# Score tiles of 16 positions of all 8 heads in place of 128 positions of one head

## The reference

```
xn  = layernorm(x)
q   = (xn @ Wq + bq).reshape(B, T, 8, 128) + pe        # T = 1024, B = 8
k,v = split(xn @ Wkv + bkv);  k = k + pe               # one head, shared by all 8
s   = where(causal, q @ k.T / sqrt(128), min)
out = (softmax(s) @ v).reshape(B, T, 1024) @ Wo
ffn = sigmoid(xr @ Wr.T) * (relu(xk @ Wk.T)**2 @ Wv.T) # xr, xk mix xn with the position before
y   = x + out + ffn
```

## Time and profile before

| | us |
|---|---|
| median of 3 runs (1758.52 to 1759.99) | 1759.03 |
| span of the profiled execution | 1756.4 |
| TensorE busy | 1686.9 (96%) |
| weight loads busy | 1624.8 (93%) |
| VectorE busy | 1244.0 (71%) |
| ScalarE busy | 1118.1 (64%) |
| GpSimd busy | 784.9 (45%) |

### The profile page before, as it was taken

The page is one execution under the profiler, slowest core; times in us unless marked ns, Lnnn a source line. Parts: engine busy times, 40 slices in busy tenths (PEclk is TensorE's granted clock), DMA queues, the critical chain, the costliest instruction groups (busy, mean ns, idle before and its releaser), DMA issues.

```text
span 1756.4 us, 41996 instructions
## 1 busy us (share of the span) xinstructions
PE 1686.9 (96%) x12982; PEld 1624.8 (93%) x12982; DVE 1244.0 (71%) x3466; ACT 1118.1 (64%) x2694; POOL 784.9 (45%) x991
## 2 busy tenths in 40 slices
PE   5999999999999998999989999899998999989999
PEld 5899988999899998999989999899998999989998
DVE  5777757777677766777767767677766777667776
ACT  4666656765566656676566766666666666666665
POOL 5544345443454434544345443454435443444434
PEclk9999999999999999999999999999999999999999
DMA  3000000000000000000000000000000000000000
GB/s 123 14 13 5 10 15 14 14 5 13 12 14 14 6 12 13 17 11 13 4 15 14 11 13 4 16 13 14 10 4 15 13 14 10 4 20 12 11 11 13
DMA packets 23586, 25.38 MB, mean 14 GB/s; under 512 B 2064, under 2 KB 22672, under 8 KB 23312
## 3 DMA queue, kind: packets, MB, share of 16 engines
q1 hardware_dynamic: 22736, 21.50, 3.9%
q10 hardware_dynamic: 576, 0.66, 0.1%
HBM read 13.77 MB, written 8.39 MB: 13 GB/s over the span
## 4 chain that ended last, share of the span: by engine, by line
PE 92%; issue 3%; DVE 2%; POOL 1%; ACT 1%; DMA 1%; SPq 0%; POOLq 0%; DVEq 0%; ACTq 0%
PE pS L741 33%; PE pO L741 22%; PE pG L741 21%; PE pT L851 15%; POOL X L348 1%; DMA X<-wq_dram 1%; DVE X L709 0%; ACT pt L464 0%; PE pS L787 0%; PE pG L787 0%; DVE pt L643 0%; DVE qtmp L588 0%; PE pG L797 0%; DVE rec L716 0%; PE pS L797 0%
## 5 line engine op out<-in xcount | busy, mean ns | idle before, releaser
L348 POOL TENSOR_SCALAR X<-X,rec 128x128 f32<-128x128 f32 (+7 forms) x518 | 385.9, 745 | 952.0 <-DVE rec L716 951.5
L741 PE MATMUL pS<-kt,qt 128*128 128x512 f32 (+5 forms) x2325 | 513.4, 348 | 0.8 <-POOL qt L332 0.8
L643 DVE TENSOR_TENSOR pt<-pT,pt 128x512 fp32r<-128x512 f32 (+3 forms) x772 | 402.7, 549 | 112.0 <-ACT pt L464 97.6
L741 PE MATMUL pO<-pt,v 128*128 128x256 f32 x3459 | 451.5, 280 | 0.0
L709 DVE CUSTOM_DVE_ANT_0 X<-pS,mask 128x128 f32<-128x128 f32 (+7 forms) x519 | 387.4, 746 | 79.9 <-PE pS L741 72.2
L741 PEld LDWEIGHTS pO<-pt,v 128*128 128x128 f32 x3459 | 436.8, 188 | 6.7
L472 ACT ACTIVATE X<-X,bias 128x128 f32<-128x128 f32 (+7 forms) x518 | 404.7, 781 | 28.8 <-DVE bias L709 28.3
L464 ACT CAST pt<-pT 128x512 fp32r<-128x512 f32 (+3 forms) x772 | 343.5, 480 | 102.7 <-PE pT L851 94.9
L741 PEld LDWEIGHTS pS<-kt,qt 128*128 128x128 f32 x2325 | 376.3, 190 | 19.2 <-POOL qt L332 1.0
L851 PE MATMUL pT<-ident,X 128*128 128x128 f32 x2308 | 343.9, 275 | 52.0 <-POOL X L348 26.8
L851 PEld LDWEIGHTS pT<-ident,X 128*128 128x128 f32 x2308 | 267.4, 141 | 86.6 <-issue 30.4
(11 more groups left out here) (90 smaller groups left out, 1583.1 us busy)
## 6 DMA issues: line engine op xcount, KB each, us to landing
xtok<-x_dram SPq DMA_DIRECT2D x36, 256.0 KB, 2.7
out_dram<-xtok SPq DMA_DIRECT2D x64, 128.0 KB, 1.7
X<-wq_dram SPq DMA_DIRECT2D x2, 512.0 KB, 8.5
X<-wo_dram SPq DMA_DIRECT2D x2, 512.0 KB, 3.9
pet<-pet_dram ACTq DMA_DIRECT2D x1, 512.0 KB, 6.5
kpos<-petok_dram SPq DMA_DIRECT2D x1, 512.0 KB, 9.2
X<-wkv_dram SPq DMA_DIRECT2D x1, 256.0 KB, 3.7
X<-wk_dram SPq DMA_DIRECT2D x1, 256.0 KB, 9.5
```

What stands on the lines that cost most here:

```text
L348: nc.gpsimd.tensor_scalar(X[:, j, 0:w], X[:, j, 0:w], rec[:, j:j + 1], 1.0, ALU.mult, ALU.mult).then_inc(normed, 1)
L643: nc.vector.tensor_tensor(pt[1][:, (s // 2) % 2, k:k + nk, half_q], pT[u % 2][:, 0:nk * P].rearrange("p (k q) -> p k q", k=nk), pt[0][:, ( ...
L741: last = nc.tensor.matmul(out, a[i], m[j], start=start and k == 0, stop=k == n - 1)
```

## The change

A step is now 16 positions (`SUB`) of all 8 heads: 128 rows again, since keys and values are shared. Step s has the width qi*128 + (s % 8 + 1)*16, so the last tile's columns are taken only as far as its own positions; from qi 4 on the two halves are half of that each. `qt` is laid out by groups of 16 positions, heads inside, so that the 128 weights of a step are contiguous; the ScalarE cast and the GpSimd subtract write it in runs of 16 elements, and `ot` likewise. A step needs the queries of all heads, and the Q units are moved ahead accordingly: all four pairs of a chunk are made in the chunk before, and before the loop for the first. GpSimd zeroes the columns between the width and the end of the tile, because the transposes still take whole blocks; then it multiplies, in turn it + 2 in place of it + 1.

The transposes stand 5 steps behind the scores, the value products 8, LEAD is 9. `X` has five rows, and the four first steps of an entry use narrow rows of their own (`Xn`), so the mask no longer waits for transposes. The keys and values get a buffer of their own (`kv`), apart from `xn`. The other fillers change turns.

The order inside a turn changes on two engines. On ScalarE the exp of it - 1 moves from behind the casts of the transposes to the front of the turn. On VectorE the reciprocal of it - 1 moves from behind the mask of it to between the subtracts and the fillers. The small triangle is built from a 128 x 8 x 16 pattern once at the start. The DMA scratch is set smaller.

```diff
 NC = T // CHUNK
 NT = T // P
 PAIRS = H // 2
+SUB = P // H
 STEPS = NT * H
 SCALE = float(D) ** -0.5
 EPS = 1e-5
 MASKED = 1e30
 HUGE = 3e38
-T_LAG = 3
-PV_LAG = 6
-XBUF = 4
+T_LAG = 5
+PV_LAG = 8
+XBUF = 5
+NARROW = 4
 MIX_AT = 12
-LEAD = 7
+LEAD = 9
 LAST_IT = STEPS + LEAD
 PER = TPC * H
 def fillers():
     at = {it: [] for it in range(LAST_IT)}
     for c in range(NC):
-        turns = {2: ("FK", c, 0), 4: ("Q", c, 3), 7: ("XT", c + 1, 0), 8: ("FV", c, 0),
-                 9: ("KV", c + 1, 0), 10: ("Q", c + 1, 0), 11: ("KT", c + 1, 0), 12: ("Q", c + 1, 1),
-                 13: ("WO", c, 0), 14: ("Q", c + 1, 2)}
+        turns = {1: ("FK", c, 0), 4: ("FR", c, 0), 5: ("XT", c + 1, 0), 6: ("FV", c, 0),
+                 7: ("KV", c + 1, 0), 8: ("Q", c + 1, 0), 9: ("KT", c + 1, 0), 10: ("Q", c + 1, 1),
+                 11: ("Q", c + 1, 2), 13: ("Q", c + 1, 3), 15: ("WO", c, 0)}
         if c == NC - 1:
-            turns = {2: ("FK", c, 0), 4: ("Q", c, 3), 7: ("XT", c + 1, 0), 8: ("FV", c, 0),
-                     9: ("KV", c + 1, 0), 11: ("Q", c + 1, 0), 12: ("Q", c + 1, 1), 13: ("WO", c, 0),
-                     14: ("Q", c + 1, 2), 15: ("KT", c + 1, 0)}
+            turns = {i: u for i, u in turns.items() if u[0] not in ("KT", "WO")} | {14: ("WO", c, 0), 15: ("KT", c + 1, 0)}
         for i, u in sorted(turns.items()):
             at[c * PER + i].append(u)
-        at[c * PER + PER + 5].append(("WO", c, 1))
     for c in range(NC):
-        at[c * PER + 6].append(("FR", c, 0))
+        at[c * PER + PER + 7].append(("WO", c, 1))
     return at
 FILL = fillers()
-START = [("XT", 0, 0), ("KV", 0, 0), ("KT", 0, 0)] + [("Q", 0, p) for p in range(PAIRS - 1)]
+START = [("XT", 0, 0), ("KV", 0, 0), ("KT", 0, 0)] + [("Q", 0, p) for p in range(PAIRS)]
+def slot_of(s):
+    return XBUF + s if s < NARROW else (s - NARROW) % XBUF
+def width(s):
+    return s // H * P + (s % H + 1) * SUB
...
-        qt = [sb(f"qt{i}", [P, 2, H, CHUNK], R) for i in range(2)]
+        qt = [sb(f"qt{i}", [P, 2, CHUNK // SUB, H, SUB], R) for i in range(2)]
...
-        bias = sb("bias", [P, XBUF])
-        total = sb("total", [P, XBUF])
-        rec = sb("rec", [P, XBUF])
+        Xn = sb("Xn", [P, NARROW, P])
+        bias = sb("bias", [P, XBUF + NARROW])
+        total = sb("total", [P, XBUF + NARROW])
+        rec = sb("rec", [P, XBUF + NARROW])
...
-            tri = mask[:, T - P:T]
-            nc.gpsimd.affine_select(out=tri, in_=tri, compare_op=ALU.is_ge, fill=MASKED,
-                                    base=0, pattern=[[-1, P]], channel_multiplier=1).then_inc(consts, 1)
+            nc.gpsimd.memset(steps_of[:, :, :], MASKED).then_inc(tri_made, 1)
+            pool.wait_ge(tri_made, 1)
+            nc.gpsimd.affine_select(out=steps_of[:, :, :], in_=steps_of[:, :, :], compare_op=ALU.is_ge, fill=0.0,
+                                    base=0, pattern=[[-SUB, H], [0, SUB]], channel_multiplier=1
+                                    ).then_inc(tri_made, 1)
+            pool.wait_ge(tri_made, 2)
+            nc.gpsimd.affine_select(out=steps_of[:, :, :], in_=steps_of[:, :, :], compare_op=ALU.is_ge, fill=0.0,
+                                    base=SUB - 1, pattern=[[SUB, H], [0, SUB]], channel_multiplier=-1
+                                    ).then_inc(tri_made, 1)
+            pool.wait_ge(tri_made, 3)
+            nc.gpsimd.affine_select(out=steps_of[:, :, :], in_=steps_of[:, :, :], compare_op=ALU.is_gt, fill=0.0,
+                                    base=0, pattern=[[SUB, H], [1, SUB]], channel_multiplier=-1
+                                    ).then_inc(tri_made, 1)
...
             def turn(b, it):
-                s = it - 1
+                s = it - 2
                 if 0 <= s < STEPS:
-
-                    w = (s // H + 1) * P
-                    j = s % XBUF
+                    w = width(s)
+                    j = slot_of(s)
                     pool.wait_ge(rec_ready, b * STEPS + s + 1)
                     pool.sem_inc(pool_passed, 1)
-                    nc.gpsimd.tensor_scalar(X[:, j, 0:w], X[:, j, 0:w], rec[:, j:j + 1], 1.0,
+                    if s % H < H - 1:
+                        nc.gpsimd.memset(x_row(s, w, (s // H + 1) * P), 0.0).then_inc(normed, 1)
+                    nc.gpsimd.tensor_scalar(x_row(s, 0, w), x_row(s, 0, w), rec[:, j:j + 1], 1.0,
                                             ALU.mult, ALU.mult).then_inc(normed, 1)
...
             def turn(b, it):
+                s = it - 1
+                if 0 <= s < STEPS:
+                    w = width(s)
+                    j = slot_of(s)
+                    act.wait_ge(masked, b * STEPS + s + 1)
+                    nc.scalar.activation(x_row(s, 0, w), x_row(s, 0, w), ACT.Exp, bias=bias[:, j:j + 1],
+                                         scale=-1.0, accum_out=total[:, j:j + 1]).then_inc(exp_done, 1)
                 first = it - PV_LAG
                 if 0 <= first < STEPS and first % 2 == 0:
                     pair = first // 2
                     act.wait_ge(pv_done, b * (STEPS // 2) + pair + 1)
-                    h = first % H
-                    if h == 0 and not (isinstance(b, int) and pair == 0):
+                    q0 = first % H * SUB
+                    if q0 == 0 and not (isinstance(b, int) and pair == 0):
 
                         act.wait_ge(filled["WO"], b * NT + first // H)
-                    nc.scalar.copy(ot[0][:, h:h + 2, :],
-                                   pO[:, 0:2 * P].rearrange("p (h q) -> p h q", h=2)).then_inc(o_hi, 1)
+                    nc.scalar.copy(ot[0][:, :, q0:q0 + 2 * SUB].rearrange("p h (t q) -> p t h q", t=2),
+                                   pO[:, 0:2 * P].rearrange("p (t h q) -> p t h q", t=2, h=H)).then_inc(o_hi, 1)
...
-                s = it - 1
-                if 0 <= s < STEPS:
-                    w = (s // H + 1) * P
-                    j = s % XBUF
-                    act.wait_ge(masked, b * STEPS + s + 1)
-                    nc.scalar.activation(X[:, j, 0:w], X[:, j, 0:w], ACT.Exp, bias=bias[:, j:j + 1],
-                                         scale=-1.0, accum_out=total[:, j:j + 1]).then_inc(exp_done, 1)
...
+                s = it - 1
+                if 0 <= s < STEPS:
+                    j = slot_of(s)
+                    dve.wait_ge(exp_done, b * STEPS + s + 1)
+                    nc.vector.reciprocal(rec[:, j:j + 1], total[:, j:j + 1]).then_inc(rec_ready, 1)
...
-                    w = (qi + 1) * P
-                    j = s % XBUF
+                    w = width(s)
+                    j = slot_of(s)
 
                     if qi < 4:
                         scores = pS[s % 2][:, 0, 0:w]
                         m = mask[:, T - w:T]
-                        o = X[:, j, 0:w]
+                        o = x_row(s, 0, w)
                     else:
                         scores = pS[s % 2][:, :, 0:w // 2]
                         m = mask[:, T - w:T].rearrange("p (a n) -> p a n", a=2)
-                        o = X[:, j, 0:w].rearrange("p (a n) -> p a n", a=2)
-                    if s >= XBUF:
-                        dve.wait_ge(t_filled, b * T_BODY + T_FIRST[s - XBUF + 1])
-                    elif not first_row:
-                        dve.wait_ge(t_filled, (b - 1) * T_BODY + T_FIRST[STEPS + s - XBUF + 1])
+                        o = x_row(s, 0, w).rearrange("p (a n) -> p a n", a=2)
                     dve.wait_ge(s_filled, b * STEPS + s + 1)
                     dve.sem_inc(dve_passed, 1)
                     nc.vector.tensor_tensor_reduce(out=o, in0=scores, in1=m, scale=SCALE, scalar=HUGE,
                                                    op0=ALU.add, op1=ALU.min,
                                                    accum_out=bias[:, j:j + 1]).then_inc(masked, 1)
-                s = it - 1
-                if 0 <= s < STEPS:
-                    j = s % XBUF
...
-                    pe.wait_ge(normed, b * STEPS + s + 1)
+                    pe.wait_ge(normed, b * N_BODY + N_FIRST[s + 1])
...
-                    qi, h = s // H, s % H
-                    c, t = qi // TPC, qi % TPC
-                    w = (qi + 1) * P
+                    qi = s // H
+                    c = qi // TPC
+                    w = width(s)
                     n = chunk_no(b, c)
                     if s % PER == 0:
                         pe.wait_ge(kt_ready, n + 1)
-                    if t == 0:
-                        pe.wait_ge(q_ready, n * H + h + 1)
+                        pe.wait_ge(q_ready, n * H + H)
                     if s >= 2 or not first_row:
                         pe.wait_ge(masked, b * STEPS + s - 1)
                     if SHARED <= s < SHARED + 2:
...
-                                       [([q[:, c % 2, h, t * P:(t + 1) * P] for q in qt],
+                                       [([q[:, c % 2, s % PER, :, :].rearrange("p h q -> p (h q)")
+                                         for q in qt],
```

74 lines of the change are left out of this document (45 added, 29 removed).

## The result

| | before | after |
|---|---|---|
| median, us | 1759.03 (3 runs, 1758.52 to 1759.99) | 2179.2 (4 runs, 2178.19 to 2180.59) |
| ratio, 95% interval | | 1.2387 (1.2368 to 1.2405) |
| span of the profiled execution | 1756.4 | 2177.1 |
| granted clock, mean of that execution | 0.992 | 0.937 |

A fourth execution of the kernel before took 3341.32 us; it is in neither the median nor the ratio. The changed kernel takes 420 us more. The prediction had the direction and the mechanism, 2013 us with a range of 1890 to 2090; the time lies 89 us above the top of the range and 166 above the forecast.

What follows compares the result with a forecast made beforehand. The prediction took TensorE to bound the kernel before, and a one-turn VectorE-ScalarE ring the changed one: 245.0 us per b, 1960 for eight, plus 50 for the start, 2010 of span, 2013 as a median; range 1890 to 2090.

Steps and rivals of the forecast that it cites:

- The ring: Mask, exp, copies, subtracts, reciprocal, fillers, next mask wait in turn across VectorE and ScalarE, closing in one turn; 202.7 us per b.
- both cross waits: VectorE idle before subtracts for ScalarE's copy, and ScalarE idle before exp for VectorE's mask; each over 150 us.
- Its price as a link: The reciprocal on VectorE between subtracts and fillers: 0.08 us a turn, 4.4 us over turns 9 to 63 of one b.
- The start: Before the loop: all four Q pairs split before step 0, about 4.5 us later, then nine turns of about 2.4; 50 us.
- the sum: All terms for one b, from turns 9 to 63, shared turns and back edge: 245.0 us, 1960 for eight.
- the nine turns shared with the next b: Small masks but large transposes and value products; TensorE needs 30.1 us, plus 1.5 of waits: 31.6.
- 202.7 + 4.1 + 3.4 + 3.2: Per b: links and fillers of turns 9 to 63, turns with TensorE longer, ScalarE's late fillers, the loop's back edge.
- The term for turns in which TensorE is the longer, "+4.1": Turns with WO's 24 matmuls ahead of scores, adding up the larger of both for each pair of turns: +4.1 us per b.
- Rival (c): Gaps drop TensorE to the 1.2 GHz level at qi 1 and 2: +21 x 8, 2180 us; chance 0.05, shared with costly strides.
- The norm: Among VectorE's fillers: priced within 21 operations of 256 columns per 16 turns, at 0.40 us each.
- Rival (a): No closed cycle, or links overlap far more; TensorE stays the bound: 1691 us as a median, 4% faster; chance 0.03.
- Edits costed at nothing: GpSimd's zeroing (0 to 354 us possible), 16-element runs in qt and ot (up to 80), triangle mask, DMA scratch: taken as 0.

Runs made afterwards that it cites:

- before_ring: Kernel before with only the exp moved first on ScalarE and the reciprocal ahead of fillers and mask on VectorE; 2012.76 us, ratio 1.144.
- both_back: Changed kernel with the exp put back behind the transposes' copies and the reciprocal back behind the mask; 1824.94 us, ratio 1.0369.
- rec_back: Changed kernel with only the reciprocal put back behind the mask on VectorE, the exp still first on ScalarE; 2143.29 us, ratio 1.2182.
- The three single edits: Each on the changed kernel: WO ahead of KV in turn 7, 2151.42 us; 12 extra matmuls before WO's wait, 2156.11; norm at front of VectorE's turn, 2131.79.
- narrow3: both_back with lags 3 and 6, LEAD 7, multiply at it - 1, WO in turns 13 and 5, last Q pair in turn 12; 1790.68 us, ratio 1.0176.
- before_table: Kernel before with only narrow3's table of fillers, all four Q units made in the chunk before; 1813.61 us, ratio 1.0299.
- ring_warm: Changed kernel with 12 extra matmuls of 256 columns ahead of WO's wait for the output subtract, in 32 places; 2156.11 us, ratio 1.2251.

## Why the prediction was right, and where it was wrong

**The ring: right.** It forecast TensorE at about 84% busy (84%), masks at qi 7 4.9 to 5.1 us apart (5.02 in the stretch shown, 5.3 over the tile with WO's wait in it), at qi 1 2.4 to 2.9 (the four masks from 1119.72 to 1128.58 are 2.95 apart, a little over; 3.4 over the tile, with WO's wait and the back edge in it), both cross waits over 150 us (342 and 743), GpSimd waited for by almost nobody (11 us in all on TensorE), and the chain through mask and exp. The two orders alone give 2012.8 (before_ring), and with both moved back 354 us go (both_back): that is the cause shown. The agreement of the 84% is partly luck: 84% of the span that was forecast is about 1690 us of work, and TensorE was busy 1819.6, part of it at the lower clock. One detail fell: the reciprocal isn't needed to close the ring, the exp's place closes it alone. Its price as a link held: 4.4 us for each b, 35 in all, against the 36 of rec_back.

**The start: nearly right.** Scores began at 27.77 us, 4.0 later (forecast 4.5), and the ninth turn at about 46.5 (forecast 50). So a b takes (2177.1 - 46.5) / 8 = 266.3 us, where the sum had 245.0. The miss, 21.3 us for each b or 170 in all, lies within it. By the masks' starts it isn't in the nine turns shared with the next b, which take 32.0 us (forecast 31.6). From the mask of turn 8 to that of turn 63 each of the later entries takes 234.0 to 234.3 us, where the sum has 202.7 + 4.1 + 3.4 + 3.2 = 213.4:

- *The term for turns in which TensorE is the longer, "+4.1", is the step that failed.* It took the larger of both engines, as though TensorE could start WO while the ring runs. The rows show it cannot: WO waits for an output subtract or, in the second half, for the sums of KV in the same bank, both of them in the ring, and then the ring waits for WO. VectorE stands for WO in 56 turns, 114.4 + 33.3 = 147.7 us or 18.5 for each b, in place of 4.1. Within it is the clock: WO is busy 34.2 us more in `pG` (158.6 against 124.4) and 26.2 in `pS` (101.1 against 74.9). Rival (c) had the clock for the narrow turns, at +168 us and a time of 2180; it came at WO instead, and the agreement with the 2179.2 measured is luck. Tiles 1 and 2 took 27.3 + 23.3 = 50.6 us, the back edge and two of WO's waits in them, where (c) has 59 and the ring 38.
- *The norm was priced at its duration before.* 66.5 - 28.1 = 38.4 us more, 4.8 for each b. No term of the sum asked whether another engine would now run beside it.

```profile
DVE xtok L692 <- PE pG L750: 114.4, 40, 4.8
...
DVE xtok L692 <- PE pS L750: 33.3, 16, 3.2
```

Together 14.4 + 4.8 = 19.2 of the 21.3, by the length of the waits and of the operation; no run takes both out of the ring at once. The three single edits took 28, 23 and 47 us out, so both places are on the path.

**Rival (a), "4% faster" without the ring: wrong.** It took the rest of the change as free, 1691. both_back, which is that case, took 1825, 134 more. The runs take the 66 us over the kernel before apart, one group of edits at a time and in one order: table +53, narrow form -23, lags and what goes with them +34 (1759 to 1760, 1813.6, 1790.7, 1824.9; the series differ by a microsecond). The prediction had named the table only for the wait for all eight heads (the last pair made in turn 13, needed in turn 16) and for fillers inside the ring. It never asked what crowding costs a kernel that TensorE bounds; it is 53 us. The narrow tiles gave 16.7 us of the 28.7 forecast: tiles 2 to 7 gave 2.9 us of the 3.6 for each b, and tile 1 took 0.6 back.

**Edits costed at nothing.** Zeroing: 62.9 us of GpSimd in 419 operations of 150 ns, no wait for it in the changed kernel; at lags 3 and 6 it shows (16.1 us of transposes' waits in narrow3). Runs of 16 elements: the output copy takes 354 ns and the split of Q 739 on average, against 371 and 741 (before_table), so nothing.

**Still open.** Whether the 6 us more of turns 8 to 15 at lags 5 and 8 come from the lags or from WO's turn: the rows name the two stands and the clock, but no run moves WO alone; in which waits the table's 53 us lie in full (transposes' wait for GpSimd's multiply rose from 26.8 to 46.8 us, which is 20 of them); and whether some table between the crowded and the late one would bring the narrow form under 1759 us. None of the kernels here beats the kernel before.

## What to carry to other kernels

When an instruction is moved in one engine's program, write down the cycle that it closes across engines and count in how many turns it closes: here one exp moved ahead of copies made two engines with 57% and 50% of work bound a kernel whose TensorE had bound it. In such a ring a wait or a slow operation of either engine is on the path, and the same edits that save 47 and 28 us in it save nothing once it is open. And a layout that needs all its inputs a stage sooner has a price in the schedule of everything that makes them, which is measured by giving the old kernel the new schedule.

## What the runs showed of the hardware

A VectorE operation from SBUF to SBUF (128 x 256, 32-bit, the norm) took 0.45 us on average before and 1.02 after. Two of them took 0.73 us together where GpSimd ran nothing beside them (before, at 77.50) and 2.31 where it was busy throughout (after, at 1009.37), and the end came 0.15 us behind GpSimd's. VectorE operations that read PSUM, like the subtracts, kept their durations (552 ns on average for L658, 549 for the same group before).

TensorE was granted 0.62 and 0.53 of its clock in the four microseconds from 1030 that follow a stand of 4.17 us, and the 24 matmuls behind the stand took 4.64 us in place of 3.12. In both_back a stand of 2.25 us, with stands of 0.99 and 0.40 us shortly before it, was followed by 0.50, and the 24 matmuls took 5.49 us. Twelve matmuls put into such stands brought the mean of WO's in `pS` from 350 back to 288 ns (ring_warm).
